# One exp and ln table, two decays ahead of the z silus, and a waiting product on GpSimd, in the projection stage of a selective scan on one Trainium2 core

## The reference, cut to what matters

```python
xs, z = jnp.split(x @ in_proj_w.T, 2, axis=-1)
xs = jax.nn.silu(conv(xs) + conv_b)              # 128 channels x 2048 tokens
dbc = xs @ x_proj_w.T                            # dt part, B rows, C rows
dt = jax.nn.softplus(dbc[..., :DT_RANK] @ dt_proj_w.T + dt_proj_b)
A = -jnp.exp(A_log)
dA = jnp.exp(dt[..., None] * A)                  # "decay", 16 states
dBu = dt[..., None] * Bm[:, :, None, :] * xs[..., None]
hs = scan(dA, dBu)                               # along the tokens
y = (einsum(hs, Cm) + xs * Dvec) * jax.nn.silu(z)
return y @ out_proj_w.T
```

## Time and profile before

| | |
|---|---|
| median of 3 runs | 646.47 us (646.43 to 647.82) |
| the profiled execution | 647.57 us, span on the core 645.8 us |
| DVE busy | 535.7 us (83% of the span) |
| PE busy | 468.8 us (73%) |
| POOL busy | 344.8 us (53%) |
| ACT busy | 242.6 us (38%) |

### The profile page before, as it was taken

One profiled execution on the slowest core, in us unless ns is written; L12 is line 12 of the kernel. 1 busy time (PEld: TensorE's weight loads), 2 busy tenths in 40 slices (PEclk: granted clock), 3 DMA queues, 4 the chain that ended last, 5 costly groups with the idle time before them and its releaser, 6 DMA issues.

```text
span 645.8 us, 6879 instructions
## 1 busy us (share of the span) xinstructions
PE 468.8 (73%) x2535; PEld 291.7 (45%) x2535; DVE 535.7 (83%) x836; ACT 242.6 (38%) x297; POOL 344.8 (53%) x197
## 2 busy tenths in 40 slices
PE   2896989987993998977777876598787888722200
PEld 2255878876982894422222322244433454512200
DVE  4999996997499343388989999999999977787897
ACT  1442413515132136778434344434444405621120
POOL 5153161456063000144699899979989817777303
PEclk9796578987797699988688899989999996855555
DMA  6410000000000001130365775546655401111100
GB/s 195 112 38 1 1 1 3 2 10 1 1 1 8 2 9 46 57 106 33 131 191 172 219 212 211 174 159 244 207 191 183 148 10 10 9 8 8 5 1 32
DMA packets 29587, 50.85 MB, mean 79 GB/s; under 512 B 16144, under 2 KB 18480, under 8 KB 29232
## 3 DMA queue, kind: packets, MB, share of 16 engines
q1 hardware_dynamic: 27760, 49.82, 24.3%
q0 software_dynamic: 1792, 0.58, 1.7%
HBM read 48.62 MB, written 1.77 MB: 78 GB/s over the span
## 4 chain that ended last, share of the span: by engine, by line
DVE 49%; PE 23%; POOL 14%; issue 6%; ACT 6%; DMA 2%; DVEq 0%; SPq 0%; POOLq 0%; ACTq 0%
DVE arena L1582 15%; POOL arena L605 9%; PE ps L676 7%; DVE ps L1572 6%; POOL arena L559 4%; PE ps L845 3%; DVE arena L1358 3%; PE ps L698 3%; DVE arena L1373 2%; PE ps L724 2%; DVE arena L1404 1%; PE ps L661 1%; PE ps L782 1%; POOL arena L552 1%; DVE arena L1356 1%
## 5 line engine op out<-in xcount | busy, mean ns | idle before, releaser
L1582 DVE TENSOR_TENSOR_SCAN arena<-arena,ps 128x1024 f32<-128x1024 f32 x64 | 144.8, 2280 | 10.2 <-POOL arena L559 2.8
L845 PE MATMUL ps<-arena,ident 128*128 128x512 f32 x256 | 130.2, 633 | 20.9 <-POOL arena L559 20.9
L534 POOL TENSOR_TENSOR arena<-arena 128x1536 f32<-128x1536 f32 (+2 forms) x16 | 65.6, 4106 | 111.0 <-DVE arena L1262 60.0
L559 POOL TENSOR_TENSOR arena<-arena 128x1024 f32<-128x1024 f32 x48 | 112.4, 2353 | 23.0 <-PE ps L845 11.9
L1110 ACT ACTIVATE arena<-arena,neg_a 128x1020 f32<-128x1020 f32 x64 | 73.1, 1145 | 120.2 <-DVE arena L1582 116.1
L676 PE MATMUL ps<-arena 128*128 128x64 f32 x576 | 81.0, 311 | 12.5 <-DVE x_tok L1290 12.5
L676 PEld LDWEIGHTS ps<-arena 128*128 128x128 f32 x576 | 80.2, 227 | 12.9 <-issue 12.9
L845 PEld LDWEIGHTS ps<-arena,ident 128*128 128x128 f32 x256 | 49.8, 201 | 71.3 <-issue 36.8
L605 POOL DMA_INDIRECT arena<-node_rows,src_idx x56 | 56.1, 1003 | 31.2 <-issue 16.8
L1572 DVE TENSOR_TENSOR ps<-arena,ps 128x1024 f32<-128x1024 f32 x48 | 58.0, 1208 | 0.3 <-PE ps L835 0.2
L1017 ACT ACTIVATE arena<-ps 128x768 f32<-128x768 f32 x48 | 37.2, 808 | 48.5 <-PE ps L724 48.5
(11 more groups left out here) (344 smaller groups left out, 744.2 us busy)
## 6 DMA issues: line engine op xcount, KB each, us to landing
arena<-state_rows SPq DMA_DIRECT2D x64, 512.0 KB, 4.3
cs<-state_rows SPq DMA_DIRECT2D x16, 512.0 KB, 4.3
arena<-dram_edges SPq DMA_DIRECT2D x2, 1024.0 KB, 8.7
arena<-dram_x SPq DMA_DIRECT2D x2, 512.0 KB, 5.0
arena<-node_rows,src_idx POOLq DMA_INDIRECT x56, 2.9
x_tok<-dram_x SPq DMA_DIRECT2D x1, 512.0 KB, 11.0
res_scratch<-x_tok SPq DMA_DIRECT2D x4, 128.0 KB, 2.0
arena<-res_scratch SPq DMA_DIRECT2D x1, 512.0 KB, 3.3
```

Source lines behind the costliest of these rows:

```text
L534: g.tensor_tensor(s_buf[i % 2][:, kk], wy[:, i, kk].unsqueeze(3).to_broadcast([P, nk, HEIGHT, WIDTH]), wx[:, i, kk].unsqueeze(2).to_broadc ...
L559: g.tensor_tensor(gg[n % 2], hh[n % 2], cs[n % GROUP], ALU.mult).then_inc(s["g_ready"], 1)
L845: m = pe.matmul(ps[:, 4 + q, :], ident[:], gg[n % 2][:, 512 * q:512 * q + 512], start=False, stop=True, skip_group_check=True)
L1582: v.tensor_tensor_scan(o, x0, x1, 0.0, ALU.mult, ALU.add).then_inc(s["scan_ready"], 1)
```

## The change

Six edits, all in the projection stage and the head of the loop.

- ACT: the exp and the negation of `A_log` (`neg_a`), which stood together ahead of the first xs silu under a table load of their own, move into the two softplus passes, one exp ahead of the ln and one negation behind it.
- ACT: an explicit load of a table that holds both exp and ln stands ahead of each softplus, in place of one load for exp and one for ln.
- ACT: decays 0 and 1 stand ahead of the four z silus; the loop starts its decays at 2.
- ACT makes the fp32 copy of the rows of direction 1; DVE makes that of direction 0 only. PE's z projection of direction 0 waits for ACT's copy too, since it writes the same PSUM banks.
- DVE: the zeroing ahead of direction 0 (`no_decay(0)`) moves up, to behind direction 0's softplus.
- POOL: the third part of direction 1 waits for `dt_ready` of direction 1.

```diff
             for d in range(2):
+                if d:
+                    g.wait_ge(s["dt_ready"], 2)
                 g.wait_ge(s["mid_ready"], d + 1)
                 g.tensor_tensor(bc3[d][0:32, :], r1[0:32, :], bc3[d][0:32, :], ALU.subtract).then_inc(s["bc_ready"], 1)
...
                         pe.wait_ge(s["rest_ready"], 2 + hf + 1)
+                        pe.wait_ge(s["rows_kept"], 2 + hf + 1)
...
-            for d in range(2):
-                f(neg_a[d][:], neg_a[d][:], ACT.Exp).then_inc(s["nega_ready"], 1)
-            for d in range(2):
-                act.wait_ge(s["nega_ready"], d + 1)
-                f(neg_a[d][:], neg_a[d][:], ACT.Copy, scale=-1.0).then_inc(s["nega_ready"], 1)
...
                     f(bc3[d][0:96, cols[hf]], banks(4 - 4 * d + 2 * hf, 2, 96), ACT.Copy).then_inc(s["hi_ready"], 1)
+                    if d:
+                        act.wait_ge(s["rows_out"], 16)
+                        f(state_rows[:, cols[hf]], banks(2 * hf, 2, 96)[C:96], ACT.Copy).then_inc(s["rows_kept"], 1)
...
+                act.preload_act_table_set(EXP_LN_TABLE)
                 act.wait_ge(s["sp_abs"], 2 * d + 2)
                 f(uu[d], uu[d], ACT.Exp, scale=-1.0).then_inc(s["sp_exp"], 1)
+                f(neg_a[d][:], neg_a[d][:], ACT.Exp).then_inc(s["nega_ready"], 1)
                 act.wait_ge(s["sp_exp"], d + 1)
                 f(sp_ln[d], uu[d], ACT.Ln, bias=1.0).then_inc(s["sp_ln"], 1)
-            silu_z(0)
-            silu_z(1)
+                act.wait_ge(s["nega_ready"], 2 * d + 1)
+                f(neg_a[d][:], neg_a[d][:], ACT.Copy, scale=-1.0).then_inc(s["nega_ready"], 1)
...
+            act.wait_ge(s["nega_ready"], 4)
+            act.wait_ge(s["dt_ready"], 1)
+            act.wait_ge(s["da_zero"], 2)
+            decay(0)
+            decay(1)
+            silu_z(0)
+            silu_z(1)
...
-                    if d and hf == 0:
-                        v.wait_ge(s["rows_out"], 16)
-                    v.tensor_copy(state_rows[:, cols], ps[C:C + 2 * DS, 4 - 4 * d + 2 * hf:6 - 4 * d + 2 * hf, :].rearrange("p b n -> p (b n)")).then_inc(s["rows_kept"], 1)
+                    if d == 0:
+                        v.tensor_copy(state_rows[:, cols], banks(4 + 2 * hf, 2, 96)[C:96]).then_inc(s["rows_kept"], 1)
...
             softplus_sum(0)
+            v.wait_ge(s["dt_ready"], 1)
+            no_decay(0)
             v.wait_ge(s["bc_ready"], 1)
             rests(1)
```

More of the change, by code:

```diff
@@ L56 @@
 BIG = 1.0e30
+EXP_LN_TABLE = "natural_log_exp_and_others"
 GROUP = 4
@@ L1095, in _, with decay @@
                     f(uu[d][:, cols[hf]], banks(4 * d + 2 * hf, 2), ACT.Abs, bias=vec[d][:, 1:2]).then_inc(s["sp_abs"], 1)
+                act.preload_act_table_set(EXP_LN_TABLE)
                 act.wait_ge(s["sp_abs"], 2 * d + 2)
                 f(uu[d], uu[d], ACT.Exp, scale=-1.0).then_inc(s["sp_exp"], 1)
+                f(neg_a[d][:], neg_a[d][:], ACT.Exp).then_inc(s["nega_ready"], 1)
                 act.wait_ge(s["sp_exp"], d + 1)
                 f(sp_ln[d], uu[d], ACT.Ln, bias=1.0).then_inc(s["sp_ln"], 1)
-            silu_z(0)
-            silu_z(1)
-            act.wait_ge(s["nega_ready"], 4)
-            for n in range(STATES):
+                act.wait_ge(s["nega_ready"], 2 * d + 1)
+                f(neg_a[d][:], neg_a[d][:], ACT.Copy, scale=-1.0).then_inc(s["nega_ready"], 1)
+            def decay(n):
                 d, c0, lo = n // (2 * DS), n // DS % 2 * HALF, 1 - n // (2 * DS)
-                if n % (2 * DS) == 0:
-                    act.wait_ge(s["dt_ready"], d + 1)
-                    act.wait_ge(s["da_zero"], 2 + d)
                 act.wait_ge(s["scan_ready"], n + 1)
@@ L1112, in _ @@
                   scale=neg_a[d][:, n % DS:n % DS + 1]).then_inc(s["da_ready"], 1)
+            act.wait_ge(s["nega_ready"], 4)
[5 more added lines that the diff above has]
+            silu_z(1)
+            for n in range(STATES):
+                if n == 2 * DS:
+                    act.wait_ge(s["dt_ready"], 2)
+                    act.wait_ge(s["da_zero"], 3)
+                if n >= 2:
+                    decay(n)
                 if n % GROUP == GROUP - 1:
@@ L1545, in softplus_sum, with no_decay @@
                 tt(dtv[d], dtv[d], sp_c[d], ALU.add).then_inc(s["dt_ready"], 1)
+            def no_decay(d):
+                first = 0 if d == 0 else SEQ - 1
+                k(v.memset(da[0].rearrange("p (b s) -> p b s", s=SEQ)[:, :, first:first + 1], 0.0))
+                v.memset(da[1].rearrange("p (b s) -> p b s", s=SEQ)[:, :, first:first + 1], 0.0).then_inc(s["da_zero"], 1)
             rests(0)
@@ L1557, in _ @@
             softplus_sum(1)
[L1561 to L1564, removed]
             def scan_state(n):
@@ L1591, in _ @@
             v.wait_ge(s["uu_ready"], 1)
-            no_decay(0)
             for n in range(STATES):
```

## The result

The changed kernel takes 649.39 us (median of 13 runs, 648.13 to 650.68), the kernel before 646.54 beside it (13 runs, 645.27 to 648.65): a ratio of 1.0037, with a 95% interval of 1.0025 to 1.0050. It is slower, by 0.4%, where a gain of 1.9 to 644.6 was forecast. The profiled execution took 649.55, its span 647.8.

What follows compares the result with a forecast made beforehand. Bound: a chain moving from engine to engine up to about 350 us, then DVE. Scan 2 gains 1.9, C product 3 1.85; the sum, 1.9 off the median 646.47, gives 644.6 us; own range 643.9 to 645.2, 8 in 10 642.6 to 646.4.

Steps and rivals of the forecast that it cites:

- `dt_ready` 3.12 earlier: End of direction 1's softplus on DVE: 300.68 in place of 303.80, 3.12 us earlier.
- The cast ran between POOL's two products: DVE's direction 1 cast was to run between POOL's two `uu` products of direction 0, 288.08 to 289.3.
- Scan 0 4.65 earlier: Loop's first scan on DVE: begins at 302.05 in place of 306.70, 4.65 us earlier.
- C product 0 0.15 later: POOL's first C product: ends at 311.8 where before 311.64; POOL gives back all of the 3.12 and 0.15 more.
- Scan 2 1.9 earlier: Scan 2 on DVE, which needs C product 0: begins at 311.9 in place of 313.78, 1.9 us earlier.
- C product 3 1.85 earlier: POOL's fourth C product, behind PE's add 1: starts at 318.9 in place of 320.75; bounds 0.95 and 2.65.
- From there each step is the one of before, shifted, up to where DVE runs alone: Loop behind C product 3: later steps keep the shift; the sum is 1.9 us off.
- whatever the head of the loop starts earlier is kept, if POOL and PE let it through: Scan stage: DVE runs at its own pace behind the chain up to about 350, so an earlier head is kept.
- if the loop behind 320 took more time than before: Scan loop after 320 us: the last of three signs that would show the prediction wrong; no size given.
- The slower rival (0.07): PE's rows between 320 and 345: each further waited-for add at low clock costs 1.7; with two, 648.0 us; chance 0.07.
- The faster rival (0.19): If PE keeps full clock at 279.54 and finds it at the adds, no scan waits for adds: 643.0 us; chance 0.19.
- 1.71 from the clear port: Part of the 3.12 at `dt_ready`: DVE's L1538 in direction 1 runs alone, 1.22 in place of 2.93.

Runs made afterwards that it cites:

- both fills: Filler matmuls on PE ahead of the experts and at the loop's three block boundaries: changed kernel 644.22 us (0.9948), kernel before 646.01 us (0.9968).
- after_late4: Changed kernel without filler, plus 4 unused matmuls on PE behind its wait for the gated product: 647.69 us, ratio 1.0009 to the kernel before.

## Why the prediction was wrong

Counted from the opening load, its steps against the trace:

- `dt_ready` 3.12 earlier: 3.07 (the start of POOL's third part, 29.22, against that of `uu`, 32.29). The cast ran between POOL's two products, as said, and took 2.14. Right.
- Scan 0 4.65 earlier: 4.57. C product 0 0.15 later: 0.17. Scan 2 1.9 earlier: 1.88. C product 3 1.85 earlier: 1.68. Right, and so was the sum as a sum over instructions: with the clock held up, the gathers start 1.84 earlier.
- **"From there each step is the one of before, shifted, up to where DVE runs alone", and "whatever the head of the loop starts earlier is kept, if POOL and PE let it through": this step failed.** It was read from busy times and the chain of waits, in which PE's clock is no step. Two falls at the block boundaries where the kernel before had one cost 1.1, which leaves 0.86 at the gathers. Then the burst ahead of the experts missed the rise of the clock: the exp of the first chunk is 7.9 later, the end 2.6. The runs with both fills show the first part, after_late4 the second. It was also the prediction's last sign of being wrong, "if the loop behind 320 took more time than before": from C product 3 to the gathers 211.00 before, 211.82 after.
- The slower rival (0.07) named the mechanism, adds at a low clock that are waited for, but at 320 to 345, where the clock was at 1.00 throughout (in the kernel before it fell twice there, 0.84 in the mean), and by whole adds of 1.7. The tail was not looked at. The Trainium skill's "TensorE: Matmul & The Clock Gate", section HAM oscillation, has bursts that are throttled again after each wait. The trace agrees in kind, not at every place: of three equal waits of PE at the block boundaries one or two led to a fall.
- The faster rival (0.19) failed at both of its conditions. PE began at 278.73, ahead of the drop, and the clock fell at about 279.6 all the same, as the prediction had taken it. At the adds, a part of the change itself held the rival off: with POOL's wait left out, add 0 is still slow, but C product 3 is 3.9 earlier and not 1.7.
- The credit was given to the wrong edits. "1.71 from the clear port" is true of `dt_ready`, and the prediction itself wrote that POOL gives all of it back; it did not ask what the kernel would do without that edit. That scan 0 waited for memsets stood in its first paragraph; that moving them gives 3.34, more than the whole change, did not.

What stays open: why a given burst or wait moves the clock and another doesn't. The runs show only that 0.9 us of shift was enough to decide it ahead of the experts.

## What to carry to other kernels

Price each edit of a bundle by itself, against the kernel without it: here one moved pair of memsets (0.06 us each) was worth 3.3 us, a wait that kept POOL out of DVE's way cost 1.4, and the rest nothing. Where PE alternates between bursts and waits, a shift upstream, here of 0.9 us, can change at each later place whether its clock falls or rises; list these places down to the end of the kernel before calling a gain kept. Fill matmuls in PE's waits take the clock out of a comparison only where the trace shows that it stays up. A delay or a fill belongs on the engine that is waited for: on another it lies in a wait and tests nothing.

## What the runs showed of the hardware

- Two profiles of the changed kernel agree within 0.02 us in every step of the table counted from the opening load, and the granted clock fell 8.5 to 8.8 behind that load in all 17 profiles. The load itself came up to 2.8 us earlier or later.
- PE busy 15.00 of 15.00 us, mostly with 64-column matmuls, stayed at 0.50 of its clock.
- When DVE took its turn between two POOL instructions, POOL's second took 3.22 and not 2.35, and a DVE pass of 1.23 beside POOL's 4.07 took 2.93 or 3.98: begun at 293.89 or 293.14, it ended 1.09 behind POOL's instruction both times.
